# First output product ahead of the last turn, a wait behind the second unit's scores, packed group counts for TensorE, casts of x behind block loops

## The chip, the cores and the metric

The kernel runs on one core of one Trainium2 chip. The metric is the device time of one launch in microseconds (us); lower is better. The engines are TensorE (PE in the profile; PEld is its weight load), VectorE (DVE), ScalarE (ACT), GpSimd (POOL) and SyncE (SP), which issues the DMAs.

## The reference

1250 nodes with 512 features pass a graph layer and then four transformer blocks whose attention runs along the same 21250 edges.

```python
msgs = feat[src]; neigh = segment_sum(msgs, dst)          # layer 0
rst = (1.0 + eps[0]) * feat + neigh
h = maximum(rst @ W1 + b1, 0.0) @ W2 + b2                 # 512 -> 1024 -> 512
x = h + feat
...
cond = silu(emb @ f_w1 + f_b1) @ f_w2 + f_b2              # from sines and cosines of a noise level
for i in range(4):
    y = cond_layer_norm(x, cond, s1_w[i], ...)            # norm, then * (1 + scale) + bias
    # 4 heads of 128: q, k, v products, scores only along the edges, softmax per source node
    x = x + attention(y) @ wo[i] + bo[i]
    y = cond_layer_norm(x, cond, s2_w[i], ...)
    x = x + relu(y @ m_w1[i] + m_b1[i]) @ m_w2[i] + m_b2[i]
...
```

Layer 0 and the blocks are followed by residual additions and layer norms. Matrix products have float32 precision here: each operand is split into a high and a low part of type fp32r, and each product takes three passes.

## The kernel before

The nodes are cut into ten tiles of 128 (the last has 98). Every product of a k-tile is three matmuls (`three_passes`), so a 128x512 result over 512 inputs is 12 matmuls. Each engine has a program of its own, written out by hand; an engine works through it in order and waits on semaphores. The order of the products of a stage comes from lists of jobs (`turned_and_dense`, `wo_m1_jobs`, `qkv_jobs`) which all engines walk: PSUM banks are dealt out in turn over eight, and a product waits until the product eight before it has been read out.

**Counting.** Layer 0 turns the edges into a dense 1250x1250 matrix of counts. VectorE and ScalarE write one-hot tiles for groups of 125 edges (`hots`, `dst_hots`), in quads of four; TensorE multiplies them, ten matmuls for each of the four (`count_block`). There are ten blocks j of destination nodes with about five quads each. How many quads a block has, and where it starts, is computed on the chip, written to `table` as packed integers and loaded into registers: tiles 0 to 3 ahead of the first quad, the rest behind it (`load_edge_tiles` with `LATER_LOADS`), on TensorE with one load more for the largest count (`most`). ScalarE writes the hot parts of the third and fourth tile of each quad; between the first quad of a block and its loop it also copies the last block's counts out of PSUM (`counts_copy`) and casts one tile of x (`x_high`).

**Attention.** The counts become a mask, and each block computes dense scores. A unit u of 40 is one node tile and one head (UNITS: pairs of tiles g, head h, tile of the pair k). For each unit TensorE computes the scores (`scores`, nine matmuls), VectorE adds the mask and takes the maximum (`mask`), ScalarE exponentiates (`exp`), TensorE turns the result (ten transposes), ScalarE and VectorE copy it out as high and low part, and TensorE weighs the values with it (`weigh`, two halves of 15 matmuls for two units together; `weigh` for the last pair is the step AV of the job list). VectorE copies a head's output into q (`head_output`), GpSimd scales it with the reciprocal sums, which SyncE has spread over all partitions by way of DRAM (`scale_head_output`, `spread_reciprocals`). `split_head_outputs` then makes high and low part of one tile of all four heads in kh, the high part on ScalarE (step OS), the low on GpSimd; these are the left operands of the WO products. kh held the keys, so this can only begin when all 40 scores are made.

**WO and what follows.** For tile t the list has WO t, then two matmuls FS and FB (scale and bias of the conditional norm) for tile t-1, and the turn T of the normed tile t-3. VectorE adds the WO product to x, takes statistics and norms; GpSimd computes the inverse deviation (`rstd_of`) and adds a bias row (`add_bias`). The step W M1 at i = 4 is the split of the next weights: a cast of 128x2048 on ScalarE and one subtraction of that size on VectorE. GpSimd's loop of this part is in `pool_block`. SyncE's part is `block_loads`: the M1 weights when all turns are made, then, when the last head's output is copied (its place in memory was v_low's), eight tiles of x and, after four of these, the last `spread_reciprocals`.

## Time and profile before

| | us |
|---|---|
| median of 3 runs | 1769.63 (1767.89 to 1771.92) |
| the profiled execution | 1772.59 |
| its span, first to last instruction | 1770.9 |
| TensorE busy | 1724.1 (97%) |
| VectorE busy | 1216.5 (69%) |
| ScalarE busy | 801.7 (45%) |
| GpSimd busy | 562.0 (32%) |

The page gives busy times and the chain of work that ended last; TensorE makes up 91% of that chain. The order of time lists merged instructions with their start, length, engine, line, operation and operands; what stands in brackets is the idle time of that engine just ahead and what ended it. The windows give each engine's busy time in a stretch, then PEclk, the clock granted to TensorE as a share of 2.4 GHz, and the DMA load. The four blocks of the network read alike; each is about 365 us long.

### The profile page before, as it was taken

How to read it: one execution, taken by the hardware profiler on the slowest of the kernel's cores; microseconds unless marked ns; L12 is line 12 of the kernel's file. 1: busy time of each engine (PE TensorE's matmuls, PEld its weight loads, DVE VectorE, ACT ScalarE, POOL GpSimd, SP SyncE). 2: the span in 40 equal slices, each digit the busy share in tenths (PEclk: the TensorE clock that was granted, in tenths of full speed). 3: DMA queues.
4: the chain of work that ended last, by engine and by line, in shares of the span. 5: the costliest groups of instructions: out<-in, count | busy, mean ns of one | idle time of the engine just before them, and what ended most of it. 6: DMA issues, size and time to landing. Idle time of an engine off the chain costs nothing.

```text
span 1770.9 us, 32299 instructions
## 1 busy us (share of the span) xinstructions
PE 1724.1 (97%) x11894; PEld 1519.9 (86%) x11894; DVE 1216.5 (69%) x2191; ACT 801.7 (45%) x1322; POOL 562.0 (32%) x880
## 2 busy tenths in 40 slices
PE   6999999999999999999999999999999999999998
PEld 6998888888998888889997888899988887999877
DVE  6997469447776866377777673677766835777676
ACT  4657432136666241256663422466644123666432
POOL 1002333303333722033336340233354502233383
PEclk9999999999999999999999999999999999999999
DMA  4002411311111302211113122112121212111221
GB/s 132 1 1 104 156 37 42 132 47 64 46 46 31 115 30 89 76 63 46 46 31 95 54 83 82 45 39 62 36 81 41 97 55 76 38 46 60 70 87 70
DMA packets 64715, 113.07 MB, mean 64 GB/s; under 512 B 15255, under 2 KB 25623, under 8 KB 64577
## 3 DMA queue, kind: packets, MB, share of 16 engines
q1 hardware_dynamic: 64576, 111.22, 19.3%
q8 instruction: 88, 1.44, 0.3%
q14 instruction: 51, 0.41, 0.1%
HBM read 89.19 MB, written 22.00 MB: 63 GB/s over the span
## 4 chain that ended last, share of the span: by engine, by line
PE 91%; DVE 4%; issue 2%; ACT 2%; DMA 1%; DVEq 0%; POOL 0%; ACTq 0%; SPq 0%; POOLq 0%
PE ps L1513 59%; PE ps L1573 15%; PE ps L1657 6%; PE ps L1465 4%; PE ps L1498 2%; PE ps L1598 2%; PE ps L1612 2%; DVE masked_s L1241 1%; DMA x<-in_x_dram 1%; DVE pT L1225 1%; ACT hot L805 0%; ACT dst_gap L801 0%; DVE x_low L1090 0%; ACT pT L984 0%; ACT s L921 0%
## 5 line engine op out<-in xcount | busy, mean ns | idle before, releaser
L1225 DVE TENSOR_TENSOR pT<-ps,pT 128x640 fp32r<-128x640 f32 (+1 forms) x320 | 243.9, 804 | 156.8 <-ACT pT L984 156.8
L1513 PE MATMUL ps<-yT,w 128*128 128x512 f32 (+1 forms) x1728 | 330.1, 352 | 0.0
L1513 PE MATMUL ps<-kh,q_parts 128*128 128x512 f32 (+3 forms) x1440 | 311.3, 360 | 9.8 <-DVE small L1241 6.5
L1513 PEld LDWEIGHTS ps<-yT,w 128*128 128x128 f32 x1728 | 280.6, 189 | 44.9
L984 ACT CAST pT<-ps 128x640 fp32r<-128x640 f32 (+1 forms) x320 | 202.3, 684 | 253.3 <-PE ps L1657 242.9
L1513 PEld LDWEIGHTS ps<-kh,q_parts 128*128 128x128 f32 (+1 forms) x1440 | 242.7, 186 | 58.1 <-issue 5.8
L1513 PE MATMUL ps<-w,kh 128*128 128x512 f32 (+1 forms) x960 | 240.6, 402 | 8.1 <-DVE x L1339 4.5
L1513 PEld LDWEIGHTS ps<-w,kh 128*128 128x128 f32 (+1 forms) x960 | 178.3, 190 | 48.4 <-DVE x L1339 5.3
L1573 PE MATMUL ps<-pT,v 128*128 128x256 f32 (+3 forms) x1600 | 215.3, 281 | 0.0
L921 ACT ACTIVATE s<-masked_s,small 128x1250 f32 (+1 forms) x156 | 211.4, 1355 | 0.0
L1573 PEld LDWEIGHTS ps<-pT,v 128*128 128x128 f32 (+1 forms) x1600 | 200.2, 190 | 0.0
L702 POOL TENSOR_SCALAR small<-small 128x1 f32<-128x1 f32 (+1 forms) x160 | 34.6, 216 | 436.7 <-ACT s L921 435.8
L950 ACT CAST yT<-ps 128x512 fp32r<-128x512 f32 x80 | 45.3, 577 | 258.6 <-PE ps L1612 258.6
L1657 PE MATMUL ps<-ident,s 128*128 128x128 f32 (+1 forms) x1560 | 150.1, 244 | 4.1 <-ACT s L921 3.9
L1657 PEld LDWEIGHTS ps<-ident,s 128*128 128x128 f32 (+1 forms) x1560 | 143.1, 139 | 5.6 <-ACT s L921 5.6
L1241 DVE CUSTOM_DVE_ANT_0 masked_s<-ps,mask 128x1250 f32<-128x1250 f32 x96 | 138.4, 1441 | 0.0
L693 POOL TENSOR_TENSOR q_parts<-q,q_parts 128x256 fp32r<-128x256 f32 (+1 forms) x80 | 53.3, 666 | 237.2 <-ACT q_parts L905 237.2
L1573 PE MATMUL ps<-pT,v_low 128*128 128x256 f32 (+3 forms) x800 | 120.6, 281 | 0.0
L1465 PE MATMUL ps<-hot 125*128 125x128 bf16 x1960 | 114.6, 222 | 5.9 <-ACT hot L805 3.0
L1465 PEld LDWEIGHTS ps<-hot 125*128 125x128 bf16 x1960 | 112.3, 99 | 8.1 <-ACT hot L805 4.5
L638 POOL TENSOR_SCALAR ve<-mv 128x1 f32<-128x1 f32 (+1 forms) x100 | 41.8, 418 | 229.4 <-DVE mv L1100 228.8
L1069 DVE TENSOR_SCALAR hot<-iota_n,edge 125x1280 bf16<-125x1280 f16 x196 | 103.1, 550 | 11.8 <-PE ps L1465 6.1
(185 smaller groups left out, 2544.6 us busy)
## 6 DMA issues: line engine op xcount, KB each, us to landing
mask<-mask_dram SPq DMA_DIRECT2D x24, 640.0 KB, 5.0
x_spill<-x SPq DMA_DIRECT2D x36, 256.0 KB
x<-x_spill SPq DMA_DIRECT2D x36, 256.0 KB, 3.9
rep<-rec_dram SPq DMA_DIRECT2D x64, 128.0 KB, 3.3
w_raw<-in_L_gnn_m_w_dram SPq DMA_DIRECT2D x8, 1024.0 KB, 6.2
mask_y<-mask_dram SPq DMA_DIRECT2D x12, 640.0 KB, 5.2
mask_dram<-mask_out SPq DMA_DIRECT2D x10, 640.0 KB, 2.9
x<-in_x_dram SPq DMA_DIRECT2D x2, 2304.0 KB
```

The costliest lines, as they stand in the source:

```text
L638: nc.gpsimd.tensor_scalar(ve[0:R, t:t + 1], mv[0:R, t, 1:2], EPS, None, ALU.add).then_inc(ve_s, 1)
L693: nc.gpsimd.tensor_tensor(q_parts[:, gh % 2, 1, 0:wd], q[:, h, g * 2 * P:g * 2 * P + wd], q_parts[:, gh % 2, 0, 0:wd].bitcast(F32), ALU.su ...
L921: nc.scalar.activation(to, masked_of(u), ACT.Exp, bias=small[0:R, u % 2, 1:2], accum_out=small[0:R, u % 2, 2:3]).then_inc(exp_done, 1)
L950: nc.scalar.copy(yT[:, 0, :, a * P:a * P + R], bank.rearrange("p (k r) -> p k r", r=P)[:, :, 0:R]).then_inc(act_out, 1)
L984: nc.scalar.copy(pT[:, 0, turned_places(gh, half), k * P:k * P + R], turn_bank(half, R)).then_inc(p_high, 1)
L1069: src_hot = nc.vector.tensor_scalar(hot[0:ET, m, 0:NP], iota_n[0:ET], edge[:, 0, bass.ds(t + m, 1)], None, ALU.is_equal)
L1225: nc.vector.tensor_tensor(pT[:, 1, places, k * P:k * P + R], turn_bank(half, R), pT[:, 0, places, k * P:k * P + R].bitcast(F32), ALU.subtr ...
L1241: nc.vector.tensor_tensor_reduce(masked_of(u), ps_flat[0:R, 0:N], masks[MASK_PLACE[t]][0:R, 0:N], 1.0, LOWEST, ALU.add, ALU.max, small[0:R ...
L1465: mine = mm(ps_flat[:, c0:c0 + P], hot[0:ET, m, i * P:(i + 1) * P], hot[0:ET, m, NP:NP + P], start=first and m == 0 and i % 4 == 0, stop=T ...
L1513: mine = mm(to, left(a), right(b), start=first and n == 0, stop=final and n == 2)
L1573: mine = mm(sums(gh, wd), left, pT[0:rows(t), b, place + t, 0:wd], start=(n == 0 and t == 0), stop=(n == 2 and t == NT - 1))
L1657: mine = nc.tensor.transpose(turn[0:rows(t), t - tiles[0], :].bitcast(F32R), s_of(u)[:, t * P:t * P + rows(t)].bitcast(F32R), ident_r[0:R, ...
```

## The change

It has these parts.

- In `attention`, TensorE issues the WO product of tile 0 in unit 39, ahead of the turn of that unit; the step AV stands behind WO 1 in the job list instead of behind WO 0. ScalarE's cast of head tiles 0 and 1 goes from unit 39 to unit 38, and GpSimd's subtraction for them ahead of one scaling and of the last reciprocal.
- TensorE's wait for all products of the stage before (`dve_out`) stands behind the scores of unit 1 instead of ahead of them.
- The last `spread_reciprocals` stands ahead of the wait for the last head's output on SyncE; GpSimd scales the last two heads at t = 3 instead of t = 5.
- The step W behind turned tiles is four subtractions of 128x512 on VectorE, one for each of i = 4 to 7. ScalarE's cast stays whole.
- The quad counts of four blocks are packed into one integer of `group_table` by six GpSimd steps on one partition, with the largest count beside them. TensorE loads these four values once, ahead of the first quad, and takes counts out by shifts; the place of a block is summed up as it goes.
- ScalarE's cast of x stands behind each block's loop instead of ahead of it.

The diff, cut to its core:

```diff
-    jobs = after(turned_and_dense("WO", "M1", "M1"), ("WO", 0, 0), ("AV", 0, 0))
+    jobs = after(turned_and_dense("WO", "M1", "M1"), ("WO", 1, 0), ("AV", 0, 0))
...
-        if i == 4:
-            jobs.append(("W", weights, 0))
+        if 4 <= i < 4 + KD:
+            jobs.append(("W", weights, i - 4))
...
                 sp.wait_ge(turned, i * U + U)
                 load_w("M1", m_w1, i)
+                spread_reciprocals(GH - 1, i)
                 sp.wait_ge(head_out, i * GH + GH)
                 for t in range(2, NT):
                     reload_x(t)
-                    if t == 5:
-                        spread_reciprocals(GH - 1, i)
...
+            nc.gpsimd.tensor_copy(four_groups[:, 0:NT], parts[:, 1, :]).then_inc(group_step, 1)
...
+            nc.gpsimd.tensor_copy(group_table[:, 0:3], two_of_four[:, 0, :]).then_inc(group_step, 1)
...
                 scale_head_output(GH - 4, i)
-                scale_head_output(GH - 3, i)
                 pool.wait_ge(mb2_in, i * 16 + 16)
                 split_head_outputs(0, i)
+                split_head_outputs(1, i)
+                scale_head_output(GH - 3, i)
                 reciprocal(U - 1, i)
-                split_head_outputs(1, i)
                 for t in range(NT + 1):
-                    if t == 5:
+                    if t == 3:
                         scale_head_output(GH - 2, i)
                         scale_head_output(GH - 1, i)
...
-                nc.scalar.copy(x_high[0:rows(j), j, :], x[0:rows(j), j, :]).then_inc(x_high_done, 1)
                 with act.Fori(1, quads) as k:
                     dst_hots(j, act.snap(first + k * HOT), act.snap(before + k))
+                nc.scalar.copy(x_high[0:rows(j), j, :], x[0:rows(j), j, :]).then_inc(x_high_done, 1)
...
-                    if u == U - 1:
+                    if u == U - 2:
                         act.wait_ge(scored, i * U + U)
                         split_head_outputs(0, i)
                         split_head_outputs(1, i)
...
                 quad(before, True)
-                if j == 0:
-                    packed.extend(load_edge_tiles(mybir.EngineType.PE, LATER_LOADS))
-                    most.append(pe.value_load(table[0:1, NT:NT + 1], min_val=1, max_val=NE // HOT + 1))
...
-            packed, most = load_edge_tiles(mybir.EngineType.PE, FIRST_LOAD), []
+            pe.wait_ge(group_step, 6)
+            pe.wait_ge(most_ready, 1)
...
+                quads = pe.snap((fours[j // 4] >> 6 * (j % 4)) & 63).with_bounds(min_val=1, max_val=NE // HOT + 1)
...
-                pe.wait_ge(dve_out, c.dve)
                 for u, (g, h, k) in enumerate(UNITS):
                     R = rows(2 * g + k)
                     if u + 1 < U:
                         scores(u + 1, i)
+                    if u == 0:
+                        pe.wait_ge(dve_out, c.dve)
                     if u >= 2:
                         weigh(u // 2 - 1, k, i)
+                    if u == U - 1:
+                        pe.wait_ge(masked, i * U + U)
+                        tile_product("WO", 0, ps[:, wo_m1.bank["WO", 0, 0], :], c).then_inc(made, 1)
                     pe.wait_ge(exp_done, i * U + u + 1)
```

TensorE at the end of attention, before. Products `ps<-w,kh` are WO, `pT,v_low` with `pT,v` is a half of a weighing, `ident,s` a turn, `film,cond` are FS and FB.

```order
L1573 MATMUL ps<-pT,v_low 128x226 x5
L1573 MATMUL ps<-pT,v 128x226 x10
L1657 MATMUL ps<-ident,s 128x98 x9
L1657 MATMUL ps<-ident,s 98x98
L1513 MATMUL ps<-w,kh 128x512 x12
L1573 MATMUL ps<-pT,v_low 128x226 x5
L1573 MATMUL ps<-pT,v 128x226 x10
L1573 MATMUL ps<-pT,v_low 128x226 x5
L1573 MATMUL ps<-pT,v 128x226 x10
L1513 MATMUL ps<-w,kh 128x512 x12
L1598 MATMUL ps<-film,cond 128x512 x2
L1513 MATMUL ps<-w,kh 128x512 x12
```

The same place in the changed kernel:

```order
L1599 MATMUL ps<-pT,v_low 128x226 x5
L1599 MATMUL ps<-pT,v 128x226 x10
L1539 MATMUL ps<-w,kh 128x512 x12
L1692 MATMUL ps<-ident,s 128x98 x9
L1692 MATMUL ps<-ident,s 98x98
L1539 MATMUL ps<-w,kh 128x512 x12
L1599 MATMUL ps<-pT,v_low 128x226 x5
L1599 MATMUL ps<-pT,v 128x226 x10
L1599 MATMUL ps<-pT,v_low 128x226 x5
L1599 MATMUL ps<-pT,v 128x226 x10
L1624 MATMUL ps<-film,cond 128x512 x2
L1539 MATMUL ps<-w,kh 128x512 x12
```

The first WO product moved ahead of the last turn, the second ahead of the last weighing.

GpSimd at the same place, before: `small` and `rec` are a unit's reciprocal, `q<-q,rep` a scaling, `kh<-q,kh` a low part of a head tile.

```order
L714 TENSOR_TENSOR q<-q,rep 128x256
L702 TENSOR_SCALAR small<-small 128x1
L704 TENSOR_TENSOR rec<-small,minus_one 128x1
L714 TENSOR_TENSOR q<-q,rep 128x226 x2
L720 TENSOR_TENSOR kh<-q,kh 128x4x128
L702 TENSOR_SCALAR small<-small 98x1
L704 TENSOR_TENSOR rec<-small,minus_one 98x1
L720 TENSOR_TENSOR kh<-q,kh 128x4x128 x2
```

GpSimd there in the changed kernel:

```order
L733 TENSOR_TENSOR q<-q,rep 128x256
L721 TENSOR_SCALAR small<-small 128x1
L723 TENSOR_TENSOR rec<-small,minus_one 128x1
L733 TENSOR_TENSOR q<-q,rep 128x226
L739 TENSOR_TENSOR kh<-q,kh 128x4x128 x2
L733 TENSOR_TENSOR q<-q,rep 128x226
L721 TENSOR_SCALAR small<-small 98x1
L723 TENSOR_TENSOR rec<-small,minus_one 98x1
```

Two low parts moved ahead of a scaling and of the last reciprocal.

TensorE at the first two quads of counting, before, `hot` being ten matmuls of one hot tile:

```order
L1465 MATMUL ps<-hot 128x128 x10
L416 TENSOR_LOAD table
L416 ISA x8
L416 TENSOR_LOAD table
L416 ISA x4
L1472 TENSOR_LOAD table
L1472 ISA x2
L1473 UNCONDITIONAL_BRANCH
L1473 ISA
L1465 MATMUL ps<-hot 128x128 x10
```

The same place in the changed kernel:

```order
L1500 TENSOR_LOAD group_table
L1500 ISA x8
L1489 MATMUL ps<-hot 128x128 x40
L1494 UNCONDITIONAL_BRANCH
L1494 ISA
L1489 MATMUL ps<-hot 128x128 x10
```

The three loads between the quads are gone, and the one ahead of the first reads the new table.

## Rows read from the trace of the kernel before

**Rows 1.** The page's busy times: engine, us, share of the span, instructions

```profile
PE 1724.1 (97%) x11894; PEld 1519.9 (86%) x11894; DVE 1216.5 (69%) x2191; ACT 801.7 (45%) x1322; POOL 562.0 (32%) x880
```

**Rows 2.** Windows: start:end, length, busy (instructions) of PE, PEld, DVE, ACT, POOL; PEclk

```profile
25.30:32.00 6.70, 5.96 (x57) 5.96 (x58) 3.35 (x9) 2.22 (x8) 0.00 (x0) 0.50 0.13 25
...
571.40:574.70 3.30, 2.95 (x7) 2.40 (x8) 1.36 (x3) 2.60 (x6) 3.22 (x5) 0.50 0.00 0
...
1667.10:1670.30 3.20, 3.02 (x7) 2.47 (x8) 1.28 (x3) 2.42 (x5) 3.09 (x5) 0.50 0.03 5
```

**Rows 3.** Order of time, TensorE, last turn: start, us, engine, line, operation [idle]

```profile
569.83 1.02 PE L1657 MATMUL ps<-ident,s 98*128 98x98 f32 x10 [0.97 <-ACT s L921]
571.75 4.40 PE L1513 MATMUL ps<-w,kh 128*128 128x512 f32 x12 [0.90 <-POOL kh L720]
...
579.34 2.89 PE L1513 MATMUL ps<-w,kh 128*128 128x512 f32 x12
582.07 0.64 PE L1598 MATMUL ps<-film,cond 96*128 96x512 f32 x2
```

**Rows 4.** Order of time, the other engines, the same stretch

```profile
566.31 0.67 POOL L714 TENSOR_TENSOR q<-q,rep 128x226 f32<-128x226 f32 x1
...
569.32 0.58 POOL L714 TENSOR_TENSOR q<-q,rep 128x226 f32<-128x226 f32 x1 [2.33 <-DMA rep<-rec_dram]
...
569.67 1.14 ACT L911 CAST kh<-q 128x512 fp32r<-128x512 f32 x2
...
570.43 1.17 POOL L720 TENSOR_TENSOR kh<-q,kh 128x512 fp32r<-128x512 f32 x1 [0.53 <-ACT kh L911]
...
579.53 0.39 DVE L1252 COPY q<-ps 128x226 f32<-128x226 f32 x1 [1.60 <-PE ps L1573]
```

**Rows 5.** Order of time, the later WO tiles, GpSimd, VectorE and TensorE

```profile
590.80 1.20 POOL L720 TENSOR_TENSOR kh<-q,kh 128x512 fp32r<-128x512 f32 x1
...
593.01 3.01 PE L1513 MATMUL ps<-w,kh 128*128 128x512 f32 x12
...
594.99 2.40 DVE L1263 TENSOR_TENSOR w<-w_raw,w 128x2048 fp32r<-128x2048 f32 x1
...
595.27 2.20 POOL L638 TENSOR_SCALAR ve<-mv 128x1 f32<-128x1 f32 x1
...
599.34 1.21 POOL L714 TENSOR_TENSOR q<-q,rep 128x226 f32<-128x226 f32 x2
600.51 1.18 POOL L720 TENSOR_TENSOR kh<-q,kh 128x512 fp32r<-128x512 f32 x1
...
601.83 2.52 PE L1513 MATMUL ps<-w,kh 128*128 128x512 f32 x10 [1.21 <-DVE x L1339]
```

**Rows 6.** Order of time, TensorE, the second attention's start

```profile
762.72 1.99 PE L1513 MATMUL ps<-kh,q_parts 128*128 128x512 f32 x9 [0.78 <-DVE v_sum L1321]
```

**Rows 7.** Order of time, the counting stage's first block

```profile
15.92 0.18 DVE L1054 COPY parts<-ps 1x30 f32<-1x30 f32 x1 [0.49 <-PE ps L1443]
...
20.81 2.51 PE L1465 MATMUL ps<-hot 125*128 125x128 bf16 x40
...
23.63 0.55 DVE L1069 TENSOR_SCALAR hot<-iota_n,edge 125x1280 bf16<-125x1280 f16 x1 [2.14 <-PE ps L1465]
...
25.65 0.42 ACT L805 ACTIVATE hot<-dst_gap 125x256 bf16<-125x256 f32 x1
...
26.04 15.30 PE L1465 MATMUL ps<-hot 125*128 125x128 bf16 x220 [2.72 <-DVE hot L1069]
```

**Rows 8.** Order of time, the next blocks; last row: TensorE's waits, whole program

```profile
39.99 0.62 ACT L831 CAST x_high<-x 128x512 fp32r<-128x512 f32 x1
...
41.71 11.34 PE L1465 MATMUL ps<-hot 125*128 125x128 bf16 x200 [0.36 <-ACT hot L805]
53.41 11.34 PE L1465 MATMUL ps<-hot 125*128 125x128 bf16 x200 [0.35 <-ACT hot L805]
...
PE ps L1465 <- ACT hot L805: 3.0, 9, 0.4
```

75 lines of the change are left out of this document (52 added, 23 removed).

## The prediction

> **What bounds the kernel now.** I read the page's busy shares first: TensorE is busy for 97% of the span [rows 1], so the other engines matter only where they make it wait or where its clock falls. The next view was the order of time of TensorE alone, read for its idle stretches, then the other engines in the same microseconds, to see what ended them. Idle time after the first matmul comes in five kinds, and the change touches each of them. (a) In each of the four attentions' ends, TensorE waits 0.97 us for the last exponential ahead of the last turn, then 0.90 us for the split head outputs ahead of the first WO product [rows 3]. (b) In the same place the granted clock reads 0.50, half of 2.4 GHz, and nowhere else in attention; all four blocks show it [rows 2]. The WO product issued there takes 4.40 us, the next one 2.89, and 2.73 to the start of the work behind it (582.07 - 579.34) [rows 3]. So the clock costs 1.51 us a block. (c) One WO product later on waits 1.21 us [rows 5]. (d) At each attention's start there is a wait of 0.78 us for the last value tile [rows 6]. (e) The counting stage loses 2.72 us in its first block, runs 6.8 us at half clock behind that [rows 2, 7], and waits nine times for ScalarE, 3.0 us in all [rows 8].
>
> **The last turn and the WO products.** The first WO product (12 matmuls) moves ahead of the last turn, the second takes its old place ahead of the last weighing. For the move to fill (a), its operands must be there at 568.87, where the weighing ends (569.83 less its 0.97 of idle) [rows 3]. ScalarE's casts of head tiles 0 and 1, 1.14 us, now stand behind the 39th unit's exponential, where ScalarE waited for a turn anyway; GpSimd's subtraction (1.17 us) comes directly behind the scaling at 566.31 to 566.98 [rows 4], so the first is done near 568.2 and the second near 569.3. That is 0.7 us of cover for the first. The second scaling, which waited for a DMA until 569.32 [rows 4], and the last reciprocal are passed by these two subtractions without being delayed by much. From 568.87 to the film matmuls at 582.07 TensorE had 13.20 us: two waits, turn, slow product, weighing, product [rows 3]. The same work in the new order has neither wait nor half clock: 13.20 - 0.97 - 0.90 - 1.51 = 9.82. What is late next: the third WO product waits for the last head's copy on VectorE, 0.39 us [rows 4], which the second product used to cover and of which now only two film matmuls stand in front. I take 0.2 us for it (bounds 0 and 0.4). 3.38 - 0.2 = 3.2 a block, **12.8 us** in four.
>
> Does the clock stay up? Half clock follows the two waits in four of four blocks; single waits of 1.21 and 0.78 us [rows 5, 6] leave it at full. With both waits gone nothing is left there to bring it down. The Trainium skill, "TensorE: Matmul & The Clock Gate", part 1, says that half rate is the default state and that activity releases it; by that rule the 1.51 us come back as well, and the trace agrees as far as the four stretches at 0.50 go. The same part says that the moment of switching shifts from run to run, which no row here can show.
>
> **The tail of the WO tiles.** The wait (c) has this cause: GpSimd works in order, and its addition on one column took 2.20 us from 595.27, beside VectorE's subtraction of whole M1 weights (2.40 us from 594.99); then the two scalings (1.21) come ahead of the subtraction for the eighth tile, which ends at 601.69, 0.14 ahead of the product at 601.83 [rows 5]. The change cuts the weight subtraction into four of 0.6 us, one a tile, and puts the two scalings two tiles earlier. That is not all gain: the subtraction for the sixth tile ended at 592.00 and its product began at 593.01 [rows 5]; 1.21 us of scaling ahead of it turns the 1.0 us to spare into 0.2 us of wait. Bounds: the whole 1.2 us comes back, or nothing does. I take 0.4 a block, **1.6 us** in four, since GpSimd has the same work in this stretch as before. The Trainium skill, "GPSIMD Engine Reference", section 1, says of the SBUF interfaces that GpSimd shares them with VectorE and contends with its instructions that read two SBUF inputs. The weight subtraction is one; by this rule four pieces hold GpSimd for as long in sum as one did, and the gain would be nearer to nothing than to 1.2; the stretched 2.20 agrees.
>
> The last head's spread moves on SyncE's queue ahead of the wait for its output and of eight reloads of x. It now waits behind the M1 load and for its own save. The reloads keep their trigger, the last head's copy, but the third WO product follows that copy directly, while before another product lay between. VectorE may take the third tile up to 1 us late; TensorE needs that only two tiles later, so I count nothing, and up to 0.4 us a block if the cover is gone.
>
> **Attention's start.** The wait for the last value tile moves behind the second unit's scores. These use banks that are free, and their other condition (the first mask) is met by then. So scores, mask, exponential and all behind them start 0.78 us sooner: **3.1 us** in four [rows 6]. The value tile's addition is over while the scores run, so the moved wait costs nothing. The two later waits of this place, for masks, stay.
>
> **Counting: the first block.** TensorE loads more table values between its first and second quad of hot tiles and comes to the second at 26.04 after 2.72 us idle [rows 7]. Now one load ahead of the first quad brings all counts, packed by six small GpSimd steps. VectorE's copy of the counts is done at 16.10 (15.92 + 0.18), and the first quad starts at 20.81 [rows 7]; even at 0.58 us a step, a far wider operation of GpSimd [rows 4], six end at 19.6. TensorE's own load then still stands ahead of the quad, so the bounds are 0 and 1 us; steps on one row of ten are nearer to nothing than to 0.58, so I take nothing. What ends last then? VectorE's first hot tile of the second quad starts at 23.63, which allows TensorE 24.4. ScalarE's part for its third group ended at 25.65 + 0.42 = 26.07; the cast of x ahead of it goes, 0.52 net of a length of 0.62 [rows 7, 8], giving 25.55. Two groups of ten come first, 1.1 us, so the quad effectively starts at 24.5. The 220 matmuls that now end at 41.34 then end at 24.5 + 220 x 0.0567 (11.34/200 [rows 8]) = 36.95: **4.4 us**, if the clock stays at full. If it falls once, for about the 3.4 us that it falls in attention, half of that returns: 2.7. The idle left is about 1.1 us in one piece, like the waits that left the clock alone; so I take 4.4.
>
> **Counting: the other blocks.** From block to block 53.41 - 41.71 = 11.70 us pass, and 200 matmuls without the wait need 11.17 (11.34 less the tail of the last, 0.17) [rows 8]. The 0.53 is ScalarE's: counts copy, cast of x, then the next hot part. The cast moves behind the block loop, where ScalarE waited 0.5 us for TensorE in any case. Gain at most 0.53, at least the 0.3 seen as idle if VectorE, whose five quads need about 11.2 us too, sets the pace. I take 0.46 x 9 = **4.1 us** (bounds 2.6 and 4.6).
>
> **Sum.** 12.8 + 1.6 + 3.1 + 4.4 + 4.1 = 26.0 us. The profiled execution took 1772.59 (span 1770.9), giving 1746.6; the median of the runs shown is 1769.63, 3.0 lower, so 1743.6 us.
>
> **Rivals.** *The clock falls all the same* at the last turn (some other cause than the two waits): 4 x 1.51 = 6.0 back, 1749.6. For: the stretch also changes engines' load. Against: four of four falls lie behind the two waits. *The clock falls in the first counting block*: 1.7 back, 1745.3; for it speaks that it did so in this place. *GpSimd is later, not earlier, in the WO tiles*: the third tile's late reload (1 us) adds to the early scalings, the sixth product waits 1.2 us and the eighth still some: the 1.6 is lost and 1.0 a block more, 1749.2. *The WO product cannot start early*: it stands in front of the last turn in TensorE's order, so if the subtraction for tile 0 ended at 571.6, as now, rather than at 568.2, the wait of 2.7 replaces both old ones and the clock may fall: most of the 12.8 goes, 1756. GpSimd's idle 2.33 us before 569.32 [rows 4] speaks against it. *Slower*: the two early scalings wait for the last head's spread, which is now queued behind the 1 MB M1 load. GpSimd reaches them near 587 in the time of before; the spread should land near 584. Each microsecond past 588 holds the subtraction of the sixth tile and TensorE; the gain is eaten from about 7 us on. At 10 us a block it would be 26.0 - 1.6 - 40 = 15.6 us slower, 1785. Nothing in the rows takes that long.
>
> **Chances.** Forecast 0.58; clock at the last turn 0.08; clock in the first block 0.15; late GpSimd 0.13; no early start 0.03; slower 0.03. The range reaches from the better bounds (counting 0.5, tail 3.2, head copy 0.8 more: 1739) to late GpSimd with the counting blocks at their lower bound and one fall of the clock (1749.2 + 1.5 + 1.7 = 1752.4). A measurement of this kernel can tell some 0.2%, 3.5 us, from no change: faster 0.95, within 0.02, slower 0.03.
>
> **What would show it.** No idle stretch between the 39th and 40th turn nor behind the latter, WO products of 2.73 us to the next work, granted clock 1.00 there. The attention's start without the 0.78. Block distance in counting near 11.2. A wait at the sixth WO product of about 0.2 us in place of that at the eighth. I am wrong if half clock remains at the last turn, if the first WO product itself waits, or if the third waits over 0.4 us.

## The result, and the profile after

The changed kernel takes **1757.94 us** (median of 4, 1756.42 to 1758.62), the kernel before 1769.53 in the same comparison. The ratio is 0.9932 (95% interval 0.992 to 0.9943). It is faster by 11.6 us, where 26.0 were forecast: the time lies above the range of 1739 to 1752.4. Later comparisons on other chips gave the kernel before medians from 1769.2 to 1771.1, so below a run is given by its ratio too where two comparisons meet.

The profiled execution took 1758.62, with a span of 1756.9. Its busy times answer to [rows 1]:

```profile
PE 1718.3 (98%) x11894; PEld 1516.8 (86%) x11894; DVE 1210.8 (69%) x2215; ACT 802.0 (46%) x1322; POOL 555.4 (32%) x887
```

**The last turn is as forecast.** TensorE's order of time, first block; compare [rows 3]:

```profile
562.84 2.94 PE L1539 MATMUL ps<-w,kh 128*128 128x512 f32 x12
565.62 0.95 PE L1692 MATMUL ps<-ident,s 98*128 98x98 f32 x10
566.40 2.99 PE L1539 MATMUL ps<-w,kh 128*128 128x512 f32 x12
...
572.58 0.64 PE L1624 MATMUL ps<-film,cond 96*128 96x512 f32 x2
573.23 3.04 PE L1539 MATMUL ps<-w,kh 128*128 128x512 f32 x12
```

No row has an idle time in brackets. From the first product's start to the film matmuls pass 9.74 us, where 9.82 were worked out. The third product follows directly.

**The stages behind and ahead of it are not.** These are windows of the changed kernel: from the first V product to the first weighing (attention's start) in blocks 1 and 2 (blocks 3 and 4 read 39.13 and 39.12), then in all four blocks from there to the first M1 product behind the WO tiles (weighings, last turn, WO tiles). Columns as in [rows 2].

```profile
362.03:401.15 39.12, 36.96 (x178) 30.19 (x177) 22.98 (x38) 14.15 (x24) 8.16 (x10) 1.00 0.23 83
723.10:763.75 40.65, 38.50 (x179) 31.40 (x177) 22.98 (x38) 14.22 (x24) 8.94 (x12) 0.96 0.23 80
...
401.15:604.17 203.02, 201.77 (x1478) 184.53 (x1477) 154.69 (x284) 115.03 (x190) 81.48 (x149) 1.00 0.19 55
763.75:966.96 203.21, 201.72 (x1478) 184.54 (x1477) 154.70 (x284) 114.96 (x189) 80.57 (x147) 1.00 0.19 55
1125.01:1332.70 207.69, 204.55 (x1478) 186.56 (x1477) 155.91 (x286) 115.04 (x190) 82.57 (x149) 0.98 0.18 54
1490.73:1695.20 204.47, 201.77 (x1479) 184.56 (x1477) 154.71 (x284) 115.05 (x190) 81.31 (x149) 1.00 0.16 51
```

The same two stretches of the first block before:

```profile
367.48:406.75 39.27, 37.08 (x178) 30.05 (x177) 22.08 (x38) 14.06 (x24) 8.16 (x10) 1.00 0.25 83
406.75:613.71 206.96, 203.57 (x1478) 186.00 (x1477) 156.10 (x283) 115.14 (x191) 83.56 (x149) 0.99 0.18 54
```

The other blocks of before read 39.25 to 39.27 and 206.83 to 206.94. So the four starts of attention *lose* 1.0 us in sum (3.1 gained in the forecast), and the four longer stretches gain 9.2 where 12.8 + 1.6 = 14.4 were wanted; block 3 is 0.8 us longer than before.

**The WO tiles.** VectorE, GpSimd and TensorE in the first block, and SyncE's queue (SPq). The first three rows are those of before, the M1 load, the reloads and the addition of the third tile; the rest is the changed kernel. Compare [rows 5]:

```profile
574.42 0.43 SPq L462 DMA_DIRECT2D w_raw<-in_L_gnn_m_w_dram  x1
579.96 1.75 SPq L509 DMA_DIRECT2D x<-x_spill  x4
585.49 0.69 DVE L1339 TENSOR_TENSOR x<-ps,x 128x512 f32<-128x512 f32 x1 [0.53 <-PE ps L1513]
...
570.14 0.44 SPq L466 DMA_DIRECT2D w_raw<-in_L_gnn_m_w_dram  x1
573.20 3.64 SPq L513 DMA_DIRECT2D x<-x_spill  x8
577.49 0.69 DVE L1363 TENSOR_TENSOR x<-ps,x 128x512 f32<-128x512 f32 x1 [2.30 <-DMA x<-x_spill]
...
582.46 1.22 POOL L733 TENSOR_TENSOR q<-q,rep 128x226 f32<-128x226 f32 x2
583.64 1.17 POOL L739 TENSOR_TENSOR kh<-q,kh 128x512 fp32r<-128x512 f32 x1
584.96 2.97 PE L1539 MATMUL ps<-w,kh 128*128 128x512 f32 x12 [0.90 <-POOL kh L739]
```

The reload of the third tile is issued 3.06 us behind the 1 MB M1 load, and VectorE can add it only 4.3 us later. In the four blocks this reload takes 4.17, 4.38, 6.06 and 5.61 us from issue to landing; before, issued 5.5 us behind the load, it took 2.64 to 2.83. VectorE also comes to it earlier, 2.0 us behind its issue instead of 5.5. Everything on VectorE and GpSimd shifts, the scalings come on top, and the sixth WO product waits. TensorE's waits for this releaser in the whole program (us in all, times, longest):

```profile
PE ps L1539 <- POOL kh L739: 7.2, 4, 2.8
```

In block 3 VectorE waited 4.20 us for the tile and TensorE 2.79, and the clock fell there:

```profile
1303.29 0.69 DVE L1363 TENSOR_TENSOR x<-ps,x 128x512 f32<-128x512 f32 x1 [4.20 <-DMA x<-x_spill]
...
1309.90:1316.60 6.70, 5.87 (x14) 4.65 (x15) 4.32 (x8) 0.00 (x0) 6.53 (x9) 0.50 0.46 110
```

**Attention's start**, second block; compare [rows 6]:

```profile
754.59 2.37 POOL L652 TENSOR_TENSOR film<-film_raw_t,film 32x1024 fp32r<-32x1024 f32 x1
755.76 1.75 DVE L1229 TENSOR_TENSOR v_low<-v_sum,v 98x512 fp32r<-98x512 f32 x1
755.80 1.94 PE L1539 MATMUL ps<-kh,q_parts 128*128 128x512 f32 x9 [0.70 <-DVE small L1261]
757.43 1.54 DVE L1245 TENSOR_TENSOR pT<-ps,pT 128x640 fp32r<-128x640 f32 x2
758.39 1.25 PE L1692 MATMUL ps<-ident,s 128*128 128x128 f32 x10 [0.65 <-DVE pT L1245]
760.40 3.51 PE L1539 MATMUL ps<-kh,q_parts 128*128 128x512 f32 x9 [0.77 <-DVE small L1261]
```

The 0.78 us wait is gone. In its place the second turn waits 0.65 us for the low part of the weights, which stood behind the last value tile's low part; that one took 1.75 us beside GpSimd's subtraction on the film table, where its like takes 0.68. It ends 0.55 us behind that subtraction (757.51 and 756.96), which keeps its own length: 2.37 us here and 2.36 before, with no low part beside it. Three waits now lie within 5.3 us, and here the clock fell behind them (3.51 us for 9 matmuls instead of 1.9).

**Counting and what follows.** TensorE's first row and the one behind its last wait in the first block, then its wait at the first H product of layer 0, and the window behind that; compare [rows 7, 8]:

```profile
21.13 1.28 PE L1489 MATMUL ps<-hot 125*128 125x128 bf16 x20
...
26.40 29.80 PE L1489 MATMUL ps<-hot 125*128 125x128 bf16 x530 [0.71 <-ACT hot L824]
...
182.48 0.47 PE L1539 MATMUL ps<-rst_high,w_low 128*128 128x512 f32 x1 [2.60 <-DVE rst_low L1188]
...
183.50:186.80 3.30, 3.30 (x9) 2.64 (x8) 3.06 (x10) 0.00 (x0) 0.00 (x0) 0.50 0.80 233
```

The stage ends at 132.92 instead of 140.92: 8.0 us, 8.5 forecast. But the H products, a step that the prediction doesn't speak of, now wait 2.60 us instead of 1.51, and the clock falls behind the wait; of the 8.0 us 5.4 are left when they end. The releaser named in the row can't be the cause: the first H product needs four low parts, and the fourth had ended 4.9 us ahead of the start of the last neighbour matmul, in before as here. What ends this wait is shown under the H products below.

### The profile page after: what moved, and what is told of

Read it like the earlier page. It is cut to its first block, busy times and chain, and to the rows that moved or that the text cites. A ratio compares the mean times of both kernels' runs of the same rounds, so it can differ in the third digit from the quotient of the medians.

```text
span 1756.9 us, 32326 instructions
## 1 busy us (share of the span) xinstructions
PE 1718.3 (98%) x11894; PEld 1516.8 (86%) x11894; DVE 1210.8 (69%) x2215; ACT 802.0 (46%) x1322; POOL 555.4 (32%) x887
## 4 chain that ended last, share of the span: by engine, by line
PE 91%; DVE 4%; issue 2%; DMA 1%; POOL 1%; DVEq 1%; ACT 0%; ACTq 0%; SPq 0%; POOLq 0%
PE ps L1539 59%; PE ps L1599 15%; PE ps L1692 6%; PE ps L1489 4%; PE ps L1524 2%; PE ps L1624 2%; PE ps L1638 2%; DVE masked_s L1261 1%; DMA x<-in_x_dram 1%; DVE hot L1089 1%; DVE pT L1245 0%; DVE v_low L1229 0%; DVE x_low L1110 0%; DMA x<-x_spill 0%; PE ps L1460 0%
## 5 line engine op out<-in xcount | busy, mean ns | idle before, releaser
L1489 PE MATMUL ps<-hot 125*128 125x128 bf16 x1960 | 110.6, 219 | 1.3 <-ACT hot L824 0.9
L1539 PE MATMUL ps<-w,yT 128*128 128x512 f32 (+1 forms) x480 | 110.7, 390 | 0.0
L642 POOL TENSOR_SCALAR ve<-mv 128x1 f32<-128x1 f32 (+1 forms) x100 | 36.3, 363 | 233.7 <-DVE mv L1120 233.7
```

The source lines that it names most:

```text
L642: nc.gpsimd.tensor_scalar(ve[0:R, t:t + 1], mv[0:R, t, 1:2], EPS, None, ALU.add).then_inc(ve_s, 1)
L1489: mine = mm(ps_flat[:, c0:c0 + P], hot[0:ET, m, i * P:(i + 1) * P], hot[0:ET, m, NP:NP + P], start=first and m == 0 and i % 4 == 0, stop=T ...
L1539: mine = mm(to, left(a), right(b), start=first and n == 0, stop=final and n == 2)
```

## The experiments

All ratios are against the kernel before, run on the same chip. Diffs are against the changed kernel where nothing else is said.

### The changed kernel again, and the reload ahead of the M1 load

> The changed kernel unchanged, for a second trace. Theory A (the waits of its profile belong to the kernel, the falls of the clock partly to chance): the wait of the sixth WO product stays at 0.9 us or more in each block, the wait of the first H product of layer 0 stays at 2.6, the wait of 0.65 us for the second turn of each attention stays; but the half-clock stretches stand in other places than at 183.5, 760.3 and 1309.9 us of the first trace. Time 1756 to 1759. Rival: the whole of the lost 14 us is chance of one execution; then waits of these three kinds differ by over 0.5 us here.

Measured: 1757.25 us, ratio 0.9917 (0.99 to 0.9933). The waits are of the same three kinds: 1.47, 0.66, 2.81 and 2.39 us at the sixth products (0.90, 1.14, 2.79 and 2.35 in the first trace), 2.38 at the first H product, 0.64 to 0.66 at the second turns. The clock fell again at the H products and at block 3's sixth product, which was not expected, and at attention's start in block 3 instead of 2. This run is the reference of the next ones.

```diff
-                load_w("M1", m_w1, i)
                 spread_reciprocals(GH - 1, i)
                 sp.wait_ge(head_out, i * GH + GH)
                 for t in range(2, NT):
                     reload_x(t)
+                    if t == 3:
+                        load_w("M1", m_w1, i)
```

> Changed kernel with the M1 weight load issued behind the reloads of x tiles 2 and 3 (and the last spread ahead of it) instead of ahead of the reloads. Theory A (the third tile of x arrives late because the 1 MB load stands ahead of it, VectorE and then GpSimd are late by that, and the early scalings add theirs): the third tile's addition no longer waits 2.3 to 4.2 us for the DMA, the wait of the sixth WO product falls from 0.9 to 2.8 us to at most 0.3, no half clock there; 4 to 9 us faster than the changed kernel, 1749 to 1754. Rival (the early scalings alone make the wait): the wait of the sixth product stays at 0.9 or more.

Measured: 1749.67 us, ratio 0.9876 (0.9859 to 0.9892), 7.6 us less. VectorE no longer waits for the DMA, and the sixth product has no idle:

```profile
572.72 0.80 SPq L513 DMA_DIRECT2D x<-x_spill  x2
573.56 0.43 SPq L466 DMA_DIRECT2D w_raw<-in_L_gnn_m_w_dram  x1
575.81 0.69 DVE L1364 TENSOR_TENSOR x<-ps,x 128x512 f32<-128x512 f32 x1 [1.10 <-PE ps L1540]
```

So the late tile is a cause and not a bystander: with the early scalings untouched, all four waits are gone. The reload now lands 2.6 to 2.7 us behind its issue in every block. Between this trace and that of the changed kernel run again the four stretches up to the first M1 product are 10.3 us shorter, but attention's starts are 2.5 us longer: of the four falls of the clock ahead of the program's end three lie there, and one at the H products.

### The value tile's low part out of the way

```diff
-                    if u == 0:
-                        v_low_part(NT - 1, i)
                     weights_low(u, i)
+                    if u == 0:
+                        v_low_part(NT - 1, i)
```

> Changed kernel with VectorE's low part of the last value tile behind the first unit's weights instead of ahead. Theory A: in the changed kernel this operation runs beside GpSimd's film subtraction, takes 1.75 us instead of 0.69, and holds the weights that the second turn waits for; out of the way, the second turn no longer waits 0.65 us, each attention gains about 0.65, 2.6 us in all. Rival: the second turn waits for the exponential anyway; no gain.

Measured: 1750.03 us, ratio 0.9881 (0.9864 to 0.9897), 7.2 us less. Second block:

```profile
751.97 2.37 POOL L652 TENSOR_TENSOR film<-film_raw_t,film 32x1024 fp32r<-32x1024 f32 x1
753.17 1.94 PE L1539 MATMUL ps<-kh,q_parts 128*128 128x512 f32 x9 [0.70 <-DVE small L1261]
754.71 0.68 DVE L1229 TENSOR_TENSOR v_low<-v_sum,v 98x512 fp32r<-98x512 f32 x1
755.18 1.03 PE L1692 MATMUL ps<-ident,s 128*128 128x128 f32 x10
```

The low part takes 0.68 again and the turn doesn't wait. The stretch of 39.1 us reads 38.2 in all four blocks, 3.7 us in sum; the rest of the 7.2 is clock. No fall of it outside the program's end is left in this trace, though the sixth products still wait (7.7 us in all) and the first H product too (2.36). Against the changed kernel run again 4.5 us of the difference of the spans lie at those two places, which this edit does not touch. Why the clock stayed up there isn't shown, so 3.7 us is what the edit itself is shown to give.

### Both together

> The changed kernel with both edits: the reload of the third and fourth tile of x ahead of the M1 load on SyncE, and the last value tile's low part behind the first low part of weights on VectorE. Alone they took 7.6 and 7.2 us off. Theory (the two are separate costs at separate places, at the sixth WO product and at the second turn of each attention): the gains add, about 1742.5 us, and this is what the prediction's sum (1743.6) left out. Rival (both mainly prevent the same falls of the clock): the gains overlap, 1746 or more. No wait over 0.3 us at a sixth WO product, no 0.65 us wait at the second turn.

Measured: **1740.92 us**, ratio 0.9839 (0.9823 to 0.9855). This is the best version of the study, 16 to 17 us below the changed kernel's two medians. The two gains add: by the ratios, which take out the difference between the chips, they are 0.0041 and 0.0036 alone and 0.0078 (13.8 us) together; by the medians 7.6 and 7.2 alone and 16.3 together. Intervals of 0.0016 either way can't tell these apart. Its trace has no fall of the clock ahead of the program's end; the traces of five of the six runs made from it below have one at the H products. One start of attention and one stretch from there to the first M1 product, and TensorE's waits that answer to those above:

```profile
719.00:757.21 38.21, 36.80 (x178) 30.14 (x177) 22.14 (x38) 14.07 (x24) 8.56 (x10) 1.00 0.25 85
1116.26:1318.11 201.85, 201.52 (x1478) 184.45 (x1477) 154.85 (x284) 115.35 (x191) 81.66 (x149) 1.00 0.20 55
...
PE ps L1540 <- DVE rst_low L1189: 2.2, 1, 2.2
```

Against before that is 1.05 us a block at the start (0.78 forecast) and 5.0 in the rest (3.6 forecast).

### TensorE's wait back in its old place

```diff
+                pe.wait_ge(dve_out, c.dve)
                 for u, (g, h, k) in enumerate(UNITS):
...
-                    if u == 0:
-                        pe.wait_ge(dve_out, c.dve)
```

> The changed kernel with TensorE's wait for the last value tile put back ahead of the second unit's scores. If moving that wait was worth the 3.1 us of the prediction: 1757.3 + 3.1 = 1760.4. Theory (the earlier scores bring the value tile's low part to stand beside GpSimd's subtraction of the film's low part, 1.75 us in place of 0.69, so that 0.65 us of the 0.78 are lost again): 0.78 - 0.65 = 0.13 a block, so 1757.8; below 1757.3 if waits packed closer together let the clock fall more often. The low part should read 0.7 us here and the 0.65 us wait should be gone.

Measured: 1754.24 us, ratio 0.9909 (0.9892 to 0.9927); the changed kernel had 0.9917 and 0.9932. So the moved wait alone was worth nothing, and perhaps cost a little: 0.78 stands where 0.65 stood, and the low part takes 0.71. The same edit on the version with both others:

> The kernel with both edits (1740.9), with TensorE's wait for the last value tile ahead of the second unit's scores again. It gives the moved wait its price once the low part of the last value tile stands out of the way. Prediction's term: 0.78 x 4 = 3.1 slower, 1744.0. The stage was 1.05 us shorter a block in the trace, not 0.78: 4.2, 1745.1. Rival (the move is worth nothing, since the two later waits swallow it): 1741.

Measured: 1746.17 us, ratio 0.987 (0.9854 to 0.9887), some 5 us slower than with the wait moved. In the traces the four starts are 4.2 us longer, and layer 0 is 1.5 longer with the fall of the clock at the H products, which this edit doesn't touch. The moved wait is worth its 3.1 us and one more, but only where nothing stands in the way of the second turn.

### The last turn's part alone

Against the kernel before: the products' and weighing's new places, the casts in unit 38, the subtractions ahead of the scaling; nothing else.

> The kernel before with the last turn's part alone: the first WO product ahead of the last turn, the weighing behind the second, the casts and subtractions of tiles 0 and 1 earlier. Spread, scalings, weight subtraction, attention's start and counting stand as before. By the prediction's term: 1771.1 - 12.8 = 1758.3. Theory (head output and reloads come some 7 us earlier relative to the M1 load, so the third tile of x is late also here, but the sixth WO product is not held by early scalings): the last turn's gain stands in full, some 1 us a block is lost in the WO tiles, 1762. If the early scalings alone made the sixth product wait, 1758 and no idle in the WO tiles but the 1.2 us of before.

Measured: 1767.31 us, ratio 0.9983 (0.9973 to 0.9992): 3.4 us, where 12.8 were forecast for this part. In its trace the last turn has no idle, and:

```profile
573.03 0.43 SPq L462 DMA_DIRECT2D w_raw<-in_L_gnn_m_w_dram  x1
576.09 1.75 SPq L509 DMA_DIRECT2D x<-x_spill  x4
580.64 0.69 DVE L1339 TENSOR_TENSOR x<-ps,x 128x512 f32<-128x512 f32 x1 [2.56 <-DMA x<-x_spill]
...
PE ps L1513 <- DVE x L1339: 8.1, 4, 2.1
```

This is 5 us short of the theory too. The eighth product waits 2.12 us (1.74 in one block) instead of 1.21 and 1.09, in two blocks an earlier one waits as well (1.63 and 0.79). The early spread and scalings are not in this kernel, so the late tile comes from the last turn's part itself. With the M1 load behind the first two reloads as above:

> The kernel before with the last turn's part alone, and with the M1 load on SyncE moved behind the reloads of the third and fourth tile of x. Without that second edit the last turn's part gave 3.4 us where 12.8 were forecast. Theory (the part itself is worth the forecast, and the reloads, which now follow the M1 load by 3 us instead of 8, take it back in the WO tiles): the third tile's addition no longer waits, the fifth and sixth WO product have no wait, and about 1770.7 - 12.8 = 1758 comes out. A wait of 2.12 us at the eighth product, where 1.21 stood before, is not covered by it: 0.9 a block may remain, 1761.5. Rival (the lost gain has another cause): 1766 or more.

Measured: 1758.76 us, ratio 0.9945 (0.9929 to 0.9962): 11.0 us by the medians (9.7 by the ratio), and the wait at the eighth product is 1.09 again in three blocks (1.88 in the last). The four stretches from the first weighing to the first M1 product are 12.9 us shorter than before. The term was right, and 7.6 of its 11.0 us hung on where the M1 load stands.

### The weight subtraction in one piece

```diff
-        if 4 <= i < 4 + KD:
-            jobs.append(("W", weights, i - 4))
+        if i == 4:
+            jobs.append(("W", weights, 0))
```

> The kernel with both edits (1740.9), but the M1 and M2 weight subtraction on VectorE is one of 128x2048 again, at the place of the first piece, instead of four of 128x512. The prediction gave the tail of the WO tiles 0.4 of the 1.2 us a block, and by the shared SBUF interface nearly nothing. Theory (four pieces let GpSimd's short steps in between, so the cut alone brings the 1.2 us back, since the kernel with both edits has no wait there): 1.2 x 4 = 4.8 slower, 1745.7, with GpSimd's one-column addition at 2.2 us and a wait at a product of WO tile seven or eight. Rival (pieces hold GpSimd as long in sum; the early scalings gave the gain): within 1 us of 1740.9.

Measured: 1746.54 us, ratio 0.9873 (0.9856 to 0.9889), 5.6 us slower than the version that it is made from (0.9839):

```profile
585.20 2.53 DVE L1286 TENSOR_TENSOR w<-w_raw,w 128x2048 fp32r<-128x2048 f32 x1
585.55 2.27 POOL L643 TENSOR_SCALAR ve<-mv 128x1 f32<-128x1 f32 x1
...
591.00 2.97 PE L1540 MATMUL ps<-w,kh 128*128 128x512 f32 x12 [0.94 <-POOL kh L740]
```

In pieces the same GpSimd step took 0.67 and three times 0.46 (583.91 and on) instead of 0.22, in sum 1.17 too long instead of 2.05, and never more than a tile's spare time at once. In each of these rows it ends some 0.08 us behind the subtraction beside it: the whole one ends at 587.73 and the step at 587.82, the first piece at 584.50 and the step at 584.58. TensorE's waits for GpSimd sum to 3.7 us here, to none there. The four stretches are 4.5 us longer; the rest of the difference is the fall of the clock at the H products, so the cut itself is worth 4.5.

### The scalings two tiles later

```diff
-                    if t == 3:
+                    if t == 5:
                         scale_head_output(GH - 2, i)
```

> The changed kernel with GpSimd's last two scalings back two tiles later (t = 5). If the early scalings hold the sixth WO product: its waits of 0.9 to 2.8 us go, the eighth waits again at most a little, and some 1.5 x 4 = 6 us come off 1757.3, 1751. If the late third tile holds it (putting the reloads first took all four waits away and left the scalings early): the wait only moves or shrinks by up to the 1.2 us of scalings, 1754 to 1757.

Measured: 1755.55 us, ratio 0.9921 (0.9904 to 0.9938), hardly different from the changed kernel. The waits moved: two at the sixth product (1.63 and 1.16), four of about 1.03 at the eighth.

> The kernel with both edits (1740.9) with the last two scalings at t = 5 again. With the third tile in time, GpSimd has its time to spare either way. Theory (the cut weight subtraction alone took the eighth product's wait, 5.6 us with the whole subtraction): the early scalings are worth nothing, 1741 within 1 us. Rival (they share the gain, as the prediction had it): an idle of 0.3 to 1.2 us a block comes back at the eighth product, 1742 to 1746.

Measured: 1743.46 us, ratio 0.9851 (0.9835 to 0.9868), against 0.9839 (0.9823 to 0.9855) for the early scalings; the intervals overlap, and no product waits in either. More than half of the difference in their spans (1741.6 and 1739.0) is a fall of the clock at the H products; the four stretches are 1.1 us longer (202.16 to 202.19 each). So the place of the scalings is worth about 1 us; the theory had nothing.

### Counting

Against the kernel before, packed group counts and moved cast alone:

> The kernel before with the counting part alone: packed group counts, and the cast of x behind each block's loop. By the prediction's two terms 4.4 + 4.1 = 8.5 us less: 1762.2. Theory (the stage gains 8.0, but TensorE's wait at the start of the H products, which ends 1.43 us behind an instruction fetch and not with the data, grows from 1.5 to some 2.6 us and the clock falls behind it for 3.4 us, 1.7 us lost): 8.0 - 1.1 - 1.7 = 5.2, 1765.5. Rival (the forecast holds and H is no part of it): 1762.

Measured: 1764.57 us, ratio 0.997 (0.9961 to 0.998): 5.2 us, the number of the theory with the H products in it. This kernel has the last turn of before, both waits of 0.97 and 0.90 in every block, yet its trace has the clock at half behind them in two blocks of four. The first two blocks there:

```profile
564.80:568.10 3.30, 2.41 (x13) 1.99 (x13) 1.36 (x3) 3.20 (x7) 3.22 (x5) 1.00 0.01 2
930.20:933.50 3.30, 3.30 (x9) 2.52 (x9) 0.19 (x2) 1.34 (x3) 2.07 (x2) 0.50 0.12 25
```

The moved cast alone:

```diff
-                nc.scalar.copy(x_high[0:rows(j), j, :], x[0:rows(j), j, :]).then_inc(x_high_done, 1)
                 with act.Fori(1, quads) as k:
                     dst_hots(j, act.snap(first + k * HOT), act.snap(before + k))
+                nc.scalar.copy(x_high[0:rows(j), j, :], x[0:rows(j), j, :]).then_inc(x_high_done, 1)
```

> The kernel before with the cast of x behind each counting block's loop alone; table loads as before. Prediction: ScalarE's part of the first block's second quad 0.52 earlier, and 4.1 us in the other nine blocks. The first block's own 4.4 needed both the loads and the cast: TensorE still comes to the second quad behind its loads near 26, but the fall of the clock there may stay. So 1769.8 - 4.1 = 1765.7, 1765.2 with the first block's cast. H products: if the packed counts' shorter code shifts the fetch, the wait is 1.5 us as before and the clock stays; if the stage's timing shifts it, it is 2.4 to 2.6 with a fall of the clock, and 1768.

Measured: 1765.81 us, ratio 0.9979 (0.9969 to 0.9988), 4.1 us. Its trace has the stage over at 133.34: 7.6 of the 8.0 us without the packed counts. These rows are this kernel's, with the table loads between its quads and the idle that they cause, and at full clock; those of before are [rows 7]:

```profile
20.58 2.50 PE L1465 MATMUL ps<-hot 125*128 125x128 bf16 x40
25.70 18.50 PE L1465 MATMUL ps<-hot 125*128 125x128 bf16 x328 [2.62 <-DVE hot L1069]
```

At 18.50/328 = 0.0564 us a matmul the 220 of the first block would end at 38.1; before they ended at 41.34. So 2.9 of the 4.4 us forecast for the first block (15.30 - 12.41) were the clock's 6.8 us at half. In the trace of the last turn's part alone, whose counting is that of before, it never fell there and the 220 took 12.45 us; in the one with the reload first it fell for 3.4 us.

The best version without the packed counts:

> The kernel with both edits (1740.9) with the group counts not packed: TensorE loads tables between its first two quads as before. By the prediction's term for the first block (4.4): 1745.3. Theory (the term was mostly the clock, which fell in the profiled execution of before for 6.8 us and in others for 3.4 or not at all; the wait itself costs 0.4 us, as the trace with the cast alone shows, and the H wait is 0.4 us shorter): 1741 to 1742, 2.6 us of idle at the second quad, H wait near 1.9.

Measured: 1742.18 us, ratio 0.9851 (0.9835 to 0.9867), against 0.9839 with them: at most some 2 us, not 4.4.

### The wait at the H products

22 semaphore increments, which do nothing but take up program, on TensorE ahead of its first product:

```diff
             pe.wait_ge(consts, 6)
+            for _ in range(22):
+                pe.sem_inc(passed)
```

> Changed kernel with 22 semaphore increments more at TensorE's start, where it is idle anyway. Theory A: the wait ahead of the first H product (1.51 us before, 2.60 after) is the loading of TensorE's next piece of program, which begins when TensorE reaches a certain place in its program; the change took some 20 instructions out ahead of that place, so the load starts later. With them put back the load starts ahead of the last neighbour matmul again and the wait is near 1.5 us; the kernel gains 1 us, up to 3 if the half clock behind that wait goes too. Rival: the wait is VectorE's or a collision with DMA; then it stays at 2.6.

Measured: 1759.09 us, ratio 0.9931 (0.9914 to 0.9948); the wait is 1.80 us instead of 2.60 or 2.38. The time is not shorter: the clock fell for 3.4 us in three places of its trace, one of them behind this wait. The profiled execution was the fastest of the four, 3.7 us below their median. On the best version the same:

> The kernel with both edits (1740.9) with 22 semaphore increments on TensorE ahead of the first product. Theory: the H products start at the later of the fetch's end plus 1.43 us and 1.76 us behind the last neighbour matmul (VectorE's last low part of their operands ends 1.37 behind it); the fetch ends near 0.5 instead of 0.9 to 1.1, the wait falls from 2.2 to 1.8. If no fall of the clock follows: 1740.4; with one in each, the same difference. Rival (the 60 increments showed an extra fetch at the program's start, 5 us): 1745 if 22 also reach it.

Measured: 1741.65 us, ratio 0.9846 (0.9829 to 0.9862); wait 1.82 where 2.18 stood, and a fall of the clock behind it. With 60 increments:

> The kernel of the run with both edits, with 60 more semaphore increments on TensorE ahead of its first matmul, which move every later place of TensorE's program 60 instructions on in the instruction memory. Theory (TensorE's wait of 2.1 to 2.6 us at the start of the H products is the end of an instruction fetch plus 1.43 us, and 22 such instructions took 0.7 to 0.8 us off it): the fetch comes before the last matmuls of the stage before, the wait falls to 1 us or less, and the fall of the clock behind it goes, 2 to 3 us less than the run with both edits, about 1740. Rival (the wait is the cast of x on VectorE): no change beyond 0.2 us.

Measured: 1746.15 us, ratio 0.9865 (0.9848 to 0.9882), 5 us slower. The wait is 1.91, no better than with 22, and the first product comes 5 us later:

```profile
PE ps L1449 <- issue: 12.5, 1, 12.5
```

The expectation of 1 us or less was wrong, and the DMA view shows why. What the traces have in common is the 16 KB instruction transfer of TensorE's own queue (q8). In the changed kernel, the last neighbour matmuls, and the transfer in the window 179.80 to 181.10:

```profile
178.61 1.28 PE L1524 MATMUL ps<-counts,x_low 128*128 128x226 f32 x10
...
q8 instruction: 1, 0.02, 4.8%
```

It ran from 179.95 to 180.94 (4.8% of 16 engines' 1.30 us is 1.0 us), and the first H product starts 1.54 us behind its end. In all nineteen traces this distance is 1.53 to 1.56 us; the expectations have 1.43, which is too short. The end of the transfer, counted from the start of the last neighbour matmul, and the wait: +0.04 and 1.31 (last turn with the reload first), +0.23 and 1.51 (before), +0.44 and 1.71 (best version without packed counts), +0.53 and 1.80 (22 increments), +0.61 and 1.89 (cast alone), +0.64 and 1.91 (60 increments), +1.31 and 2.57 (counting alone), +1.33 and 2.60 (changed). So the whole wait goes with this transfer, and 60 increments brought it no earlier than 22. How short the wait could become isn't known; VectorE's low part that ends 1.36 us behind the last neighbour matmul's start, named in an expectation as the bound, is the fifth, and this product needs four. Most of the shift comes with the packed counts. Ahead of the H products TensorE's program leaves one of two branches (`If`, `Else`) that hold the neighbour matmuls; whether that decides where the transfer starts was not tried, and how to place it without a loss elsewhere stays open.

## Why the prediction was wrong, step by step

**Right.** The last turn: no idle, 9.74 us where 9.82 were worked out, the head copy nowhere over 0.2 us, the clock up in all four. The measured gain of that part, with its side effect removed, is 11.0 of 12.8 us by the medians and 12.9 in the trace. The counting blocks: of the 7.6 us less in the trace of the cast alone 2.9 are clock and 0.3 an earlier second quad, which leaves 4.4 against the 4.1 forecast. The 0.78 us of attention's start are there for the taking (1.05 in the end).

**The step that failed most** is the sentence on the third tile of x: "VectorE may take the third tile up to 1 us late; TensorE needs that only two tiles later, so I count nothing, and up to 0.4 us a block if the cover is gone." The tile came 2.3 to 4.2 us late, and with the load behind it 7.6 us came back. The text saw that the third WO product follows the head copy directly, but kept the reload's length of before. What had changed was its neighbour on the queue: before, the M1 load was issued 5.5 us ahead of the reloads (574.42 and 579.96); now it is issued 3.1 us ahead, since the head output comes sooner behind the last turn, and the reload lands 4.2 to 6.1 us behind its issue instead of 2.6 to 2.8, in each block 0.8 to 1.0 us behind the load itself. A rival named the mechanism (the late tile with the early scalings, the sixth product waits 1.2 us) with a chance of 0.13, and put it at 1749.2; its waits were 0.90 to 2.79 and its clock fell once. The forecast and this rival differed by the length of one DMA that no row of before showed so near behind the load. But the trace of before has the load itself, 6.3 us from issue to landing (574.42 to 580.72), and the bound should have come from it: a tile issued 3 us behind it can land with it.

**The second** is in attention's start: "The value tile's addition is over while the scores run, so the moved wait costs nothing." True of the addition. But the paragraph looked at TensorE's conditions only. Starting the scores 0.78 us earlier also moved VectorE's low part of that value tile to stand beside GpSimd's film subtraction, 1.75 us instead of 0.68, ahead of a low part that TensorE's second turn needs. Putting the low part behind the weights' gave 7.2 us, of which 3.7 are this stage's own and the rest falls of the clock, part of them elsewhere. In place of +3.1 the part gave nothing.

**The third** is a stage that the sum doesn't contain: the H products, 1.1 us of wait and 1.5 of clock. The trace of before had a wait of 1.5 there whose named releaser had done its part long before. The end of an instruction transfer moved from 0.23 to 1.33 us behind the last neighbour matmul's start, and the wait with it.

**The fourth** is a size: the 4.4 us of the first counting block. 2.9 of them were the clock, at half for 6.8 us in the profiled execution. The text carried its 26.0 us from this execution to the median by taking 3.0 off both. But executions of before with a mean clock of 0.994 took 1772.5 to 1773.5 and those with 0.997 took 1767.6 to 1769.2: the 3.0 *are* clock, and a gain of clock can't be taken from the median twice. The last turn's term holds 6.0 us of clock that not every execution loses either: with the turn of before, the trace of counting alone lost it in two blocks of four. The changed kernel's profiled execution lies only 0.7 above its median, so of the 14.0 us between the two profiled executions 11.6 are left between the medians.

**The fifth** erred to the other side: the tail of the WO tiles at 0.4 of 1.2 us, because by the shared interface four pieces would hold GpSimd as long as one. The Trainium skill, "GPSIMD Engine Reference", section 1, says that GpSimd shares its SBUF interfaces with VectorE and contends with its instructions that read two SBUF inputs. The trace agrees that each piece stretches the step beside it. What the argument left out is that a short step waits at most for the rest of one piece (0.45 us and three times 0.24, where the whole one cost 2.05), and that a delay below the tile's spare time costs nothing. Cutting was worth 4.5 us in four blocks and the earlier scalings about 1, more than the bound of 1.2 a block, and in the changed kernel the late tile hid it.

From the trace of before to that of the changed kernel: counting 8.0, H products -2.6, attention's start -1.0, last turn and WO tiles 9.2, and 0.4 in the rest make 14.0 us. With the two edits the same sum is 31.9 (1770.9 - 1739.0): 20.0 in the last turn and WO tiles, 4.3 at attention's start, 7.4 in layer 0, 0.2 in the rest. The forecast's mechanisms were all there; two collisions of moved work, one with another load and one with another engine's work, took about half of the gain (0.0161 of ratio in the best version, 0.0068 to 0.0083 in the changed kernel).

## What to carry to other kernels

When a step is moved earlier, follow what it releases on the other queues: a small reload that used to come 5.5 us behind a 1 MB load and now comes 3 us behind it took 4.2 to 6.1 us to land instead of 2.6 to 2.8, and the cure is to issue it first. Look also for which two instructions on VectorE and GpSimd come to stand side by side that did not before. And before a profile's gain is carried to the median, take the clock's share out of it: compare the mean clock of the profiled execution with those of the other executions.

## What the runs showed of the hardware

- Beside each other, a VectorE instruction that reads two operands from SBUF and a GpSimd instruction that reads SBUF cost time, and in both cases here the one that started later paid: VectorE's 98x512 subtraction took 1.75 us instead of 0.68 beside a 32x1024 one on GpSimd that kept its 2.37 us; GpSimd's step on one column took 2.27 us instead of 0.22 beside a 128x2048 subtraction on VectorE that had started 0.35 us ahead of it. VectorE's 128x640 subtraction that reads one operand from PSUM took 0.83 and 0.82 us beside the same GpSimd instruction (from 751.77 in the best version), and its median in the whole program is 0.82. The rule of the Trainium skill named above speaks of this difference, and these rows agree.
- The clock at half appeared, ahead of the program's end, in steps of 3.4 or 6.8 us and not in every execution. Behind the same pair of waits (0.97 and 0.90 us, 1 us of work between) it fell in four of four blocks in two traces and in two of four in another. Behind three waits of 0.64 to 0.77 us within 5.3 us it fell in one of four blocks in four traces and in three of four in another. With two waits of 0.70 and 0.64 us in the same place it did not fall in any of 28 blocks of seven traces. Behind the single wait at the H products it fell in 12 of 19 traces, with waits of 1.80 to 2.60 us; it stayed up in three with 1.89, 2.18 and 2.36, and in the four with 1.31 to 1.71.
- A reload of 256 KB issued 3.1 us behind a 1 MB load on the same queue landed 3.8 to 6.1 us after its issue, in twelve blocks of three traces; issued 5.5 us behind such a load (before), or ahead of it (twelve blocks of three traces), 2.6 to 2.8 us.
- TensorE's program comes by DMA in transfers of 16 KB, one for about every 256 of its records where it runs straight (256 on average over the 75 distances from 230 us on in the trace of before). The Trainium skill, "Advanced Engine Details and Errata", part "ISA Cache", says 16 KB and 256 instructions to a line, and the trace agrees. At the H products such a transfer ended 0.04 to 1.33 us behind the start of the last neighbour matmul, and TensorE stood for 1.31 to 2.60 us; the waits view put it down to VectorE, since only the DMA view shows the transfer.
